# First attention of a fused transformer kernel: PSUM handed over one head at a time instead of two

## The reference, cut to what matters

```python
qkv = x @ qkv_w + qkv_b                               # x: (16, 512, 128)
q, k, v = jnp.moveaxis(qkv.reshape(b, n, 3, H, D), 2, 0)   # H = 16, D = 8
attn = jnp.einsum('bnhd,bmhd->bhnm', q, k) * scale
attn = jax.nn.softmax(attn, axis=-1)
out = jnp.einsum('bhnm,bmhd->bnhd', attn, v).reshape(b, n, c)
out = out @ proj_w + proj_b
```

## Time and profile before

| | |
|---|---|
| device time, median of 3 runs | 3276.28 us (3265.56 to 3277.72) |
| profiled execution, span from first to last instruction | 3286.4 us |
| first attention's products L960 and L970 | from 433.6 to 1292.3 us of the span |
| busy share of the whole span | PE 88%, DVE 77%, ACT 54%, POOL 28% |
| busy in that attention's stretch 774.0 to 823.8 (49.8 us) | PE 48.01, DVE 42.25, ACT 36.90, POOL 9.23 us |

### The profile page before, as it was taken

One profiled execution on the slowest core, in us unless ns is written; L12 is line 12 of the kernel. 1 busy time (PEld: TensorE's weight loads), 2 busy tenths in 40 slices (PEclk: granted clock), 3 DMA queues, 4 the chain that ended last, 5 costly groups with the idle time before them and its releaser, 6 DMA issues. The chain is left out here.

```text
span 3286.4 us, 46340 instructions
## 1 busy us (share of the span) xinstructions
PE 2885.2 (88%) x15778; PEld 1733.9 (53%) x15778; DVE 2521.8 (77%) x6150; ACT 1771.8 (54%) x2711; POOL 920.1 (28%) x885
## 2 busy tenths in 40 slices
PE   6999869999999997999976698899899999989853
PEld 4666523444444433666654465566566656656432
DVE  6998778888888861899967898776466687797765
ACT  3545317777777774455445456464344555655444
POOL 2212122111111101122101455565223323434233
PEclk9999959999999995999985789899899999999875
DMA  4434332212212201343420000000000000000000
GB/s 130 101 83 104 81 106 86 98 54 95 87 66 95 86 22 43 88 105 88 95 53 1 1 14 20 13 26 20 33 7 14 14 14 7 14 7 26 7 7 26
DMA packets 71604, 167.20 MB, mean 51 GB/s; under 512 B 8793, under 2 KB 9417, under 8 KB 67145
## 3 DMA queue, kind: packets, MB, share of 16 engines
q1 hardware_dynamic: 69192, 160.04, 16.9%
q10 hardware_dynamic: 2176, 4.19, 0.3%
HBM read 120.68 MB, written 43.52 MB: 50 GB/s over the span
## 5 line engine op out<-in xcount | busy, mean ns | idle before, releaser
L710 DVE TENSOR_REDUCE att_mx<-att_pair 128x2 f32<-128x1024 f32 x512 | 617.2, 1220 | 122.7 <-PE att_pair L960 122.6
L886 ACT ACTIVATE att_pt<-att_pair 128x1024 f32<-128x1024 f32 x512 | 522.7, 1025 | 226.1 <-PE att_pair L970 223.8
L982 PE MATMUL att_o<-att_pt,att_vx 128*32 128x256 f32 x4096 | 329.1, 406 | 10.1 <-ACT att_oT L892 5.1
L960 PE MATMUL att_pair<-att_k,att_q 32*128 32x512 f32 x1024 | 266.6, 524 | 50.5 <-DMA att_k<-att_spread_k 14.9
L970 PE MATMUL att_pair<-att_q,att_k 32*128 32x512 f32 x1024 | 261.7, 512 | 0.0
L970 PEld LDWEIGHTS att_pair<-att_q,att_k 32*128 32x128 f32 x1024 | 97.2, 188 | 190.7 <-issue 165.2
L960 PEld LDWEIGHTS att_pair<-att_k,att_q 32*128 32x128 f32 x1024 | 98.4, 191 | 140.3 <-ACT att_pt L886 92.5
L460 ACT ACTIVATE ffnA_h<-ffnA_up,b 128x512 f32<-128x512 f32 x144 | 98.9, 688 | 131.2 <-PE ffnA_up L105 130.7
L460 ACT ACTIVATE ffnB_h<-ffnB_up,b 128x512 f32<-128x512 f32 x144 | 98.7, 686 | 130.4 <-PE ffnB_up L105 129.9
L982 PEld LDWEIGHTS att_o<-att_pt,att_vx 128*32 128x32 f32 x4096 | 90.8, 110 | 140.1 <-issue 120.2
L1908 ACT ACTIVATE att1k_sq<-att1k_k 128x512 f32<-128x512 f32 x128 | 76.2, 595 | 163.0 <-PE att1k_k L105 162.8
(11 more groups left out here) (535 smaller groups left out, 7691.5 us busy)
## 6 DMA issues: line engine op xcount, KB each, us to landing
ffnA_weights<-ffnA_weights SPq DMA_DIRECT2D x128, 256.0 KB, 5.1
att_q<-att_spread_q SPq DMA_DIRECT2D x16, 1024.0 KB, 4.9
att_k<-att_spread_k SPq DMA_DIRECT2D x16, 1024.0 KB, 4.8
att_spread_q<-att_qhi SPq DMA_DIRECT2D x32, 256.0 KB, 2.5
att_spread_k<-att_khi SPq DMA_DIRECT2D x32, 256.0 KB, 3.3
twk_hi<-ffnB_weights SPq DMA_DIRECT2D x32, 256.0 KB, 3.8
twk_lo<-ffnB_weights SPq DMA_DIRECT2D x32, 256.0 KB, 5.1
tgk_hi<-ffnB_weights SPq DMA_DIRECT2D x32, 256.0 KB, 6.1
```

The costliest lines, as they stand in the source:

```text
L710: v.tensor_reduce(top[b % 2][:, t, h:h + 2], pair("s", k)[:, :].rearrange("p (h n) -> p h n", h=2), AX, ALU.max, negate=True).then_inc(mx, 1)
L886: a.activation(pt[k % 8][:, :, :].rearrange("p h n -> p (h n)"), pair("t", k)[:, :], ACT.Exp, scale=scale).then_inc(p_, 1)
L960: last = pe.matmul(pair("s", k)[:, (j - j0) * 512:(j - j0 + 1) * 512], qb[b % 3][r, u, t * P:(t + 1) * P], kb[b % 3][r, u, :], start=True, ...
L982: last = pe.matmul(obank[j * BLOCK:(j + 1) * BLOCK, cols], vxb[b % 3][:, t, 4 * u + j, :], pt[(2 * g + j // 2) % 8][:, j % 2, cols], start ...
```

## The change

The six banks become two rings of three single banks: `s` for first scores, `t` for second scores. Each head's product gets a bank, its own wait and its own signal; DVE and ACT take one head (512 columns) at a time, two instructions in a step where there was one. A first score's bank waits only for DVE's maximum three heads earlier, a second score's bank only for ACT's exponential three heads earlier. `uses`, `use_number`, `pair` and `pair_free` go. `WEIGHED` puts both halves of a tile together, in places 4, 6, 8 and 10. Counts of the semaphores double.

```diff
-WEIGHED = {4: ((0, 0),), 5: ((0, 1),), 6: ((1, 0),), 7: ((1, 1),), 8: ((2, 0),), 9: ((2, 1), (3, 0)), 10: ((3, 1),)}
+WEIGHED = {4: ((0, 0), (0, 1)), 6: ((1, 0), (1, 1)), 8: ((2, 0), (2, 1)), 10: ((3, 0), (3, 1))}
...
-    banks = [mem.ps(f"pair{i}", 1024) for i in range(3)]
+    sbanks, tbanks = [mem.ps(f"s{i}") for i in range(3)], [mem.ps(f"t{i}") for i in range(3)]
...
         def maxed(k):
             b, u, t, j = place(k)
             h = 4 * u + j
-            v.wait_ge(s_, k + 1)
-            v.tensor_reduce(top[b % 2][:, t, h:h + 2], pair("s", k)[:, :].rearrange("p (h n) -> p h n", h=2), AX, ALU.max, negate=True).then_inc(mx, 1)
+            for n in (2 * k, 2 * k + 1):
+                v.wait_ge(s_, n + 1)
+                v.tensor_reduce(top[b % 2][:, t, h + n % 2:h + n % 2 + 1], sbanks[n % 3][:, :], AX, ALU.max, negate=True).then_inc(mx, 1)
...
         def exps(k):
-            a.wait_ge(t_, k + 1)
             if k >= 8:
                 a.wait_ge(w_, 2 * ((k - 8) // 2 + 1))
             if k == 0:
                 a.wait_ge(fill, 32)
-            a.activation(pt[k % 8][:, :, :].rearrange("p h n -> p (h n)"), pair("t", k)[:, :], ACT.Exp, scale=scale).then_inc(p_, 1)
+            for n in (2 * k, 2 * k + 1):
+                a.wait_ge(t_, n + 1)
+                a.activation(pt[k % 8][:, n % 2, :], tbanks[n % 3][:, :], ACT.Exp, scale=scale).then_inc(p_, 1)
...
         def scores(k):
...
-            pair_free(pe, "s", k)
             for j in (j0, j0 + 1):
-                r = slice(BLOCK * j, BLOCK * (j + 1))
-                last = pe.matmul(pair("s", k)[:, (j - j0) * 512:(j - j0 + 1) * 512], qb[b % 3][r, u, t * P:(t + 1) * P], kb[b % 3][r, u, :], start=True, stop=True)
-            last.then_inc(s_, 1)
+                n, r = 2 * k + j - j0, slice(BLOCK * j, BLOCK * (j + 1))
+                if n >= 3:
+                    pe.wait_ge(mx, n - 2)
+                pe.matmul(sbanks[n % 3][:, :], qb[b % 3][r, u, t * P:(t + 1) * P], kb[b % 3][r, u, :], start=True, stop=True).then_inc(s_, 1)
...
         def again(k):
...
-            pair_free(pe, "t", k)
             for j in (j0, j0 + 1):
-                r = slice(BLOCK * j, BLOCK * (j + 1))
-                last = pe.matmul(pair("t", k)[:, (j - j0) * 512:(j - j0 + 1) * 512], kb[b % 3][r, u, t * P:(t + 1) * P], qb[b % 3][r, u, :], start=True, stop=True)
-            last.then_inc(t_, 1)
+                n, r = 2 * k + j - j0, slice(BLOCK * j, BLOCK * (j + 1))
+                if n >= 3:
+                    pe.wait_ge(p_, n - 2)
+                pe.matmul(tbanks[n % 3][:, :], kb[b % 3][r, u, t * P:(t + 1) * P], qb[b % 3][r, u, :], start=True, stop=True).then_inc(t_, 1)
...
         def weigh(w, t, h):
...
-            pe.wait_ge(p_, 2 * g + 2)
+            pe.wait_ge(p_, 4 * g + 4)
```

More of the change, by code:

```diff
@@ L625, in attn0 @@
     xg = lambda b: X[:, b, :, :]
[L626 to L629, removed]
     def place(k):
@@ L634, in place @@
         return b, n // 8, n % 8 // 2, n % 2 * 2
[L636 to L643, removed]
     def uses_of_misc():
@@ L714, in maxima @@
             rows = mtb[:, :, :].rearrange("p t (j r) -> p t j r", j=4)
-            v.wait_ge(mx, STEPS * (b + 1))
+            v.wait_ge(mx, 2 * STEPS * (b + 1))
             if b:
@@ L821, in operands @@
             if b >= 3:
-                sp.wait_ge(t_, STEPS * (b - 2))
+                sp.wait_ge(t_, 2 * STEPS * (b - 2))
             sp.dma_start(qb[b % 3][:, :, :].bitcast(F32).rearrange("p u n -> p (u n)"), spread_q.rearrange("j r n -> (j r) n")).then_inc(dq[b % 3], 16)
```

## The result

The changed kernel takes 3315.69 us (median of 4 runs, 3307.48 to 3327.78) against 3270.92 for the kernel before, run beside it: a ratio of 1.0141, interval 1.0114 to 1.0169. I had forecast 3243 us and a range of 3205 to 3295. The profiled execution has a span of 3311.1 us.

What follows compares the result with a forecast made beforehand. The bound was PE's in-order list, with a wait for ACT in every second step. Common steps -53, first 42 steps +11, last 42 +9 gave -33 us on the runs' median 3276.3: 3243 us, range 3205 to 3295.

Steps and rivals of the forecast that it cites:

- the first stretch: First 42 steps, set by DVE: extra maxima instructions cost 2.5 us, the stalls the rest; +11 us, at least 2.5.
- the stalls: First 42 steps: DVE, buffered by three heads instead of six, idles during PE's other pieces; 6.4 us long, 2.4 short.
- The rival in which DVE takes over: Common steps: single-bank maxima don't overlap, so DVE sets 48.7 us a block; 3291 us, up to 3305; chance 0.16.
- ACT's term: Common block: 64 exponentials at 0.60 us plus 4.2 other work, 42.4 us, below PE's floor.
- the common steps' block: Block of 32 in the 469 common steps: 46.0 us, gaining 3.6 a block, 53 us in all.
- a floor of 44.4: PE's floor for a common block: two-step loop of 2.62 us, 41.9 a block, plus other pieces, 1.3 and 1.2.
- What little buffering costs: Common block: lumps of DVE's and ACT's other pieces exceed spare time; about a third taken, 1.6 us a block.
- Weighing in pairs: Common steps: four double weighs in eight steps, 4.00 us against 4.42; saves 1.7 us a block.
- The clock's rival: Common steps: single-bank pauses drop PE's clock; slower by over 0.5% from 165 us at half clock; chance 0.10.
- the gate: Common even step: a second score waits for ACT's exponential until 1.19 us after the odd step's products start.
- My own loop: Two common steps with a double weigh: 1.19 wait, 0.43 products, 1.00 weigh; 2.62 us, 41.9 a block.
- The last stretch: Last 42 steps, only second scores, mostly at half clock: +13.7 less 4.6 for hidden short pieces; +9 us, 0 to +14.

Runs made afterwards that it cites:

- six_banks: Changed kernel, but first scores use all six banks in turn in the first 42 steps and second scores in the last 42; 3282.77 us, ratio 1.0074.
- half_maxima: Changed kernel, but DVE takes each head's maximum over the first 256 of 512 columns, leaving out half that work; 3262.85 us.
- before_out: Kernel before, with only ACT's copy of the bank o put before the exponentials of its step; 3286.56 us, ratio 1.0056.
- out_first: Changed kernel, but ACT copies the finished bank o before the exponentials of its step, not after; 3307.45 us, ratio 1.0129.
- six_out: six_single_out with the change's table put back, both halves of a tile weighed together; 3275.43 us, ratio 1.0023.
- weigh_only: Kernel before with only the new WEIGHED table, halves weighed in pairs, PSUM still in three shared pairs; 3291.42 us, ratio 1.008.
- six_single_out: Changed kernel with the old WEIGHED table, six banks for one kind of scores at both ends, early copy of o; 3237.43 us, ratio 0.988.
- before_look2: Kernel before, unchanged, profiled once more; span 3274.9 us.

## Why the prediction was wrong

**What bounds the kernel before** was read rightly, and the forecast of the first stretch was right to a microsecond (+11 against +11.8), with its two parts: six banks at the ends take back 8.3 us, where I had put 8.8 on the stalls.

**Durations.** A maximum takes 0.681 us and the next starts 0.598 later (four in 2.47 to 2.50 us); I had 0.684 and 0.596. The rival in which DVE takes over, because maxima don't overlap, is out. By this cadence 32 more instructions added 32 x (2 x 0.598 - 1.132) = 2.0 us to a block of DVE's. The Trainium skill (Perfetto Trace Analysis, Optimizing Scalar/DVE Operations) has some 125 ns per instruction, by which it would have been 4.0, an estimate; the measured cadence decides. ACT's term was too large: I took 0.60 for each exponential and 42.4 us a block, but they start 0.49 apart, and ACT is busy 38.4.

**The step that failed is the common steps' block: 46.0 us forecast, 49.5 measured at full clock.** Over 469 steps that is 51 of the 68 us by which the common part missed; the clock has the other 17. The 46.0 were a floor of 44.4 and 1.6 for little buffering. In the terms of that sum:

- *What little buffering costs* was taken as 1.6 us, a third of its upper end, because each engine's floor allowed catching up. By subtraction it was some 4: 49.5 is 5.1 over the floor, and 0.8 of that is the copy below. This remainder holds all that the sum left out. One part is shown: DVE's cast beside POOL's addition takes 0.90 us instead of 0.27, and the period behind it 3.5 instead of 2.77. A period without any other piece took 2.77 us where I had 2.62, at most 2.4 over 16 periods. And halving both readers' work gives 2.0 us more than the two alone, so time lost at one gate isn't caught up at the other. How the 4 us divide among these is not shown.
- *The copy of the bank `o`* was missing. I looked at what ACT's other pieces cost ACT, not at who waits for them: the opening `weigh` of each unit now comes 0.35 to 0.5 us before ACT is done. Moving it gave 0.8 us a block.
- *Weighing in pairs* was booked as a saving of 1.7 us a block, since it drops one change in PE's list per two steps. PE's busy time did fall (44.2 us a block, against 46.6 with the same rings and single weighings), but the single `weigh` had been the work that covers the gate, and the same rings with single weighings take 47.7 us a block. My own loop has no saving in it when worked out for the old table too. There the two steps take 1.19 + 0.43 + 0.57 = 2.19 us, and 2.44 where a double stands in the odd step: 9.01 for eight steps, 36.0 a block. The other pieces add 8.4, less what of them fits into the wait that is left: at most 44.4, which is what pairs come to. I worked it out only for the new table.

**The clock's rival came true in part.** I gave it 0.10 and asked for 165 us at half clock before it would decide. In the first profile of the changed kernel the clock stood at 0.50 for the first 20 us of the common steps, where it had risen after 14, and fell four times later, for 41 us in all; the second profile had six falls. Blocks with falls took up to 52.8 us instead of 49.5. At 49.5 a block, 469 steps are 725.5 us, and they took 742.2. The difference of 17 us is about what the forecast's own price (3 us in 10) gives for these 61 us at half clock, and `six_banks`, with the same list there and two falls, took 729.2. So the rings with pairs are level with the kernel before at full clock and lose the common part's +15 us by the clock. The end of that rival was summed too low: 469 steps at 4.08 in place of 2.87 us for two would add 284 us, some 3527 and not 3480. The Trainium skill (TensorE: Matmul & The Clock Gate, A second HAM failure mode: psum-queue depth-cycling) describes a kernel in which PE pauses between groups while PSUM banks turn and the clock goes up and down. The trace agrees as far as the clock goes up and down, with 0.96 in place of 0.99 over the common part; that the turning of the banks is the reason isn't shown here, since `half_maxima` has the same rings and pairs and no fall in its common part, and `before_out`, with the old buffers, has ten.

**The last stretch** was forecast at +9; the averages of three profiles before and two after give about +12, with a spread as large as that. That they are near each other is in part luck.

What stays open: which pattern in PE's list makes the clock fall. Pairing isn't the whole of it. The same list fell two, four and six times (`six_banks` and the two profiles of the changed kernel); with the early copy, pairs fell eleven and ten times (`out_first`, `six_out`). `weigh_only` has pairs and fell twice in 746 us, `before_out` has singles and fell ten times, `six_single_out` has singles and the early copy and fell once. A rule that sorts these was not tested. Nor was the rival that DVE's long cast is a part of what pairing costs: all kernels with pairs have it (0.87 to 1.33 us, or as long a wait in the instruction behind it), and those with rings and singles don't (0.36 to 0.37). Moving POOL's addition would tell.

## What to carry to other kernels

When a wait is to be split off an in-order list, work out the loop for the old and the new order of the work around it: a small product that looks like a cost (a change of the array, a separate start) may be what covers a round trip to another engine. Rings of three single banks need all their neighbours to be on time; halve one reader's work, then both, to see whether two gates take turns. When a change shifts the engines against each other, compare the durations of the unchanged instructions too. And before crediting an engine's pause to one wait, look at the granted clock behind it: the last 42 steps took 67.6 to 79.1 us in profiles of one and the same kernel, by the clock.

## What the hardware showed unexpectedly

- A stretch that PE fills with 42 steps of second scores and weighings ran at full clock in `before_out` (49.8 us at 1.00) and mostly at half in the kernel before (79.1 us at 0.61). With the late copy PE stands there four times for 1.65 to 1.69 us in front of a `weigh`, with the early one for at most 0.70. The first of these waits, where the products' time grows from 0.64 to 1.08 us behind it:

```profile
1220.89 0.64 PE L982 MATMUL att_o<-att_pt,att_vx 128*32 128x256 f32 x8
1221.46 0.51 PE L970 MATMUL att_pair<-att_q,att_k 32*128 32x512 f32 x4
1223.65 1.08 PE L982 MATMUL att_o<-att_pt,att_vx 128*32 128x256 f32 x8 [1.69 <-ACT att_oT L892]
```

- A wait like that doesn't bring the fall each time. In `before_look2` the same first wait ended at 1225.42 and the clock fell only at 1234.9, at the end of the second one; and `out_first`, whose waits for banks are shorter (up to 0.75 us), fell in its last stretch as well.
- Once down, the clock stayed down for 13.6 and for 44.4 us, although PE was busy nearly all of that time:

```profile
1223.50:1237.10 13.60, 13.45 (x84) 4.39 (x84) 0.55 (x2) 7.07 (x8) 0.00 (x0) 0.50 0.02 6
1240.50:1284.90 44.40, 42.71 (x250) 15.38 (x242) 2.33 (x7) 23.32 (x25) 0.00 (x0) 0.50 0.00 1
```

- A DVE cast of 64 columns took 0.27 us in the kernel before and 0.90 in the changed one. In every block at full clock it ended 0.07 to 0.08 us after POOL's addition into `X`, beside which it stood; in `out_first`, where both began together, it took 1.33 us against the addition's 1.28.
- An exponential over 512 columns takes 0.598 us, but the next ACT instruction starts about 0.49 later (four in 2.06 us); over 1024 columns it was 1.025 and 1.00 (two in 2.03 us). Two instructions in place of one cost ACT next to nothing here.
